# Attention scores made twice: row maxima first, then transposed scores with the maximum as a 97th row

## The reference, cut to what matters

```
q      = einsum('bld,dhk->blhk', x, Wq)             # 16 heads of 64
latent = einsum('bld,dc->blc', x, Wkv_down)         # 32 latent columns
k      = einsum('blc,chk->blhk', latent, Wk_up)
v      = einsum('blc,chk->blhk', latent, Wv_up)
attn   = einsum('bqhd,bkhd->bhqk', q, k) / sqrt(64)
attn   = softmax(where(key <= query, attn, lowest), axis=-1)
y      = einsum('bhqk,bkhd->bqhd', attn, v)
out    = einsum('bqhd,hdo->bqo', y, Wout)
```

## Time and profile before

| | |
|---|---|
| median of the runs (lowest, highest) | 3225.33 us (3221.89, 3227.55) |
| span of the profiled execution, first to last instruction | 3058.8 us |
| what lies around the span, median less span | 166.5 us |
| busy: PE, PEld, DVE, ACT, POOL | 84%, 68%, 66%, 59%, 28% |
| attention, first score matmul to last write of x | 60.8 to 1230.0 us of the span |

### The profile page before, as it was taken

One profiled execution on the slowest core, in us unless ns is written; L12 is line 12 of the kernel. 1 busy time (PEld: TensorE's weight loads), 2 busy tenths in 40 slices (PEclk: granted clock), 3 DMA queues, 4 the chain that ended last, 5 costly groups with the idle time before them and its releaser, 6 DMA issues.

```text
span 3058.8 us, 77303 instructions
## 1 busy us (share of the span) xinstructions
PE 2564.5 (84%) x26192; PEld 2090.3 (68%) x26193; DVE 2019.8 (66%) x5025; ACT 1803.4 (59%) x4422; POOL 853.6 (28%) x1042
## 2 busy tenths in 40 slices
PE   3899898989898998897997189999999987988990
PEld 2777777777777777776886166666766765776880
DVE  2677676767666776786665656666676666875664
ACT  2777777777777777563554155555556554654550
POOL 0000000000000000575566233424233224774660
PEclk9999999999999999776999598998999986768995
DMA  5221111112111210111322300000000000112225
GB/s 147 49 49 44 44 43 44 43 46 51 44 43 44 51 47 20 53 45 54 82 81 75 96 2 2 2 2 2 2 2 2 2 2 22 45 54 72 82 78 168
DMA packets 139323, 140.27 MB, mean 46 GB/s; under 512 B 30540, under 2 KB 105425, under 8 KB 138864
## 3 DMA queue, kind: packets, MB, share of 16 engines
q1 hardware_dynamic: 122096, 101.67, 13.2%
q0 software_dynamic: 16896, 34.12, 3.3%
HBM read 45.85 MB, written 40.54 MB: 28 GB/s over the span
## 4 chain that ended last, share of the span: by engine, by line
PE 55%; DVE 16%; issue 9%; ACT 9%; SPq 5%; DMA 4%; DVEq 1%; POOL 1%; ACTq 0%; POOLq 0%
PE psum L457 5%; PE psum L426 5%; PE psum L492 4%; SPq L412 3%; DVE state L1717 3%; PE psum L1514 3%; ACT probs L446 3%; PE psum L1137 3%; PE psum L1111 2%; DVE neg_max L435 2%; PE psum L1112 2%; PE psum L1562 2%; PE psum L1113 2%; DMA y<-y_tok 2%; PE psum L543 2%
## 5 line engine op out<-in xcount | busy, mean ns | idle before, releaser
L446 ACT ACTIVATE probs<-psum,neg_max 128x512 f32<-128x512 f32 (+3 forms) x1024 | 539.5, 538 | 244.7 <-DVE neg_max L435 242.6
L435 DVE TENSOR_REDUCE neg_max<-psum 128x1 f32<-128x512 f32 (+3 forms) x1024 | 457.3, 483 | 54.8 <-PE psum L427 25.8
L426 PE MATMUL psum<-ls,qs 96*128 96x512 f32 (+3 forms) x1024 | 383.6, 400 | 115.1 <-ACT probs L446 103.5
L457 PE MATMUL psum<-ident,probs 128*128 128x128 f32 x2560 | 431.4, 284 | 2.8 <-ACT probs L446 0.8
L324 POOL TENSOR_TENSOR rstd<-var_eps,half_neg 128x4 f32<-128x4 f32 x32 | 40.5, 1267 | 1115.3 <-DVE var_eps L320 1115.3
L426 PEld LDWEIGHTS psum<-ls,qs 96*128 96x128 f32 x1024 | 199.9, 195 | 219.2 <-ACT probs L446 164.3
L476 DVE COPY probs_t<-psum 128x512 f32<-128x512 f32 (+1 forms) x384 | 230.3, 600 | 147.5 <-PE psum L457 140.5
L1250 POOL DMA_INDIRECT y_tok<-yb,xb x272 | 267.3, 983 | 207.7 <-issue 116.9
L457 PEld LDWEIGHTS psum<-ident,probs 128*128 128x128 f32 x2560 | 275.9, 145 | 25.8 <-ACT probs_t L472 9.7
L914 POOL DMA_INDIRECT x_slot<-pay,pos_i x256 | 255.9, 1000 | 92.4 <-issue 77.2
L427 PE MATMUL psum<-causal_r,ident_r 128*128 128x128 f32 x1024 | 236.8, 244 | 0.0
(11 more groups left out here) (320 smaller groups left out, 6638.8 us busy)
## 6 DMA issues: line engine op xcount, KB each, us to landing
qs<-q_h SPq DMA_DIRECT2D x512, 64.0 KB, 2.0
xb<-x_slot SPq DMA_DIRECT2D x272, 66.0 KB, 1.8
qs<-q_l SPq DMA_DIRECT2D x256, 64.0 KB, 2.0
y<-y_tok SPq DMA_DIRECT2D x32, 512.0 KB, 3.8
y_tok<-yb,xb POOLq DMA_INDIRECT x272
x_sb<-in_x SPq DMA_DIRECT2D x16, 256.0 KB, 5.5
x_slot<-pay,pos_i POOLq DMA_INDIRECT x256, 2.3
out<-x_sb SPq DMA_DIRECT2D x16, 256.0 KB, 3.0
```

Of the source, the lines that this page charges most:

```text
L426: pe.matmul(o[:, at:at + n], q, ls[par][0:3 * LD, 0:n], start=(at == 0), stop=False, skip_group_check=True)
L435: last = dve.tensor_reduce(neg_max[:, par, h, qt:qt + 1], bank[u % 3][:, at:at + (qt + 1) * P], AX.X, ALU.max, negate=True)
L446: last = act.activation(probs[:, u % 3, c], bank[u % 3][:, c], ACT.Exp, bias=neg_max[:, par, h, qt:qt + 1], accum_out=row_sum[:, par, h, q ...
L457: last = pe.transpose(bank[3 + u % 2][:, c:c + P], probs[:, u % 3, c:c + P], ident[:, :])
```

## The change

The scores are now computed twice, in both orders.

- First as before, but only for the maximum: scores of unit u+20 (`AHEAD`), in two PSUM banks, without the mask matmul. One VectorE instruction adds the mask from SBUF, negates, reduces to minus the maximum, and writes the masked scores back to PSUM (L440; it is an instruction and an accumulator read).
- At (g,5) the maxima of the next group are transposed (L449), copied to SBUF (L455), and one DMA puts them into `qs` as row 96, the 97th; row 96 of `ls` is all ones.
- Then the keys-by-queries product with that row (L473, three banks) gives transposed scores less their maximum. ScalarE's exp writes them straight to `probs_t` (L483), one instruction a unit, with no bias and no row sum. GpSimd sets the masked half of each diagonal block to zero (`mask_gpsimd`, one a unit).
- The transposes of the probabilities, the copies of both engines and ScalarE's accumulator reads are gone. Values are matmuls of up to 512 columns instead of 128. Row sums come from a second such set, with ones as the stationary operand (L517). They are copied, transposed, inverted, spread out by GpSimd, transposed back and multiplied in (L530 to L562).
- The query items move to `PROJ_AT`: item 0 at (1,0), 1 at (1,2), 2 at (1,8), 3 at (2,8), 4 at (3,8), and 5 at (0,0) of the batch itself.
- Semaphores are shared where their uses do not meet, and the constants of the mask are made later. The other three stages keep their instructions.

The core of the diff:

```
-            o = bank[u % 3]
-                pe.wait_ge(s["s_exp"], b * UPS + u - 2)
+            o = bank[u % 2]
+            positive(pe, "s_max", b * UPS + u - 1)
             for qt, at in UNIT_TILES[k]:
                 n = (qt + 1) * P
-                pe.matmul(o[:, at:at + n], q, ls[par][0:3 * LD, 0:n], start=(at == 0), stop=False, ...)
-                last = pe.matmul(o[:, at + qt * P:at + n], ident_r[:, :], causal_r[:, :], start=False, stop=True, ...)
+                last = pe.matmul(o[:, at:at + n], qs[0:KEYS, h, qt * P:(qt + 1) * P], ls[par][0:KEYS, 0:n],
+                                 start=(at == 0), stop=True, skip_group_check=True)
...
+                last = dve.tensor_tensor_reduce(out=bank[u % 2][:, at:at + n], in0=bank[u % 2][:, at:at + n], in1=causal[:, L - n:L],
+                                                scale=-1.0, scalar=-MASKED, op0=ALU.add, op1=ALU.min,
+                                                accum_out=neg_max[:, g % 2, qt, j:j + 1])
...
+        def max_sync(sp, b, g):
+            sp.wait_ge(s["mx_out"], done)
+            sp.dma_start(qs[KEYS:KEYS + 1, g * HG:(g + 1) * HG, :].bitcast(F32),
+                         max_t[0:HG, :].bitcast(F32)).then_inc(s["mx_dma"], 16)
...
+        def keys_tensor(pe, b, par, u):
+            o = bank[2 + u % 3]
+            if u % GU == 0:
+                pe.wait_ge(s["mx_dma"], (b * G + h // HG + 1) * 16)
+            positive(pe, "s_exp", b * UPS + u - 2)
+            for kb, at in KEY_TILES[k]:
+                n = L - kb * P
+                last = pe.matmul(o[:, at:at + n], ls[par][0:KEYS + 1, kb * P:(kb + 1) * P], qs[0:KEYS + 1, h, kb * P:L], ...)
+            last.then_inc(s["k_mm"], 1)
...
-                last = act.activation(probs[:, u % 3, c], bank[u % 3][:, c], ACT.Exp, bias=..., accum_out=row_sum[...])
+            act.activation(probs_t[:, g % 2, j, UNIT_AT[k]:UNIT_AT[k] + UNIT_COLS[k]], bank[2 + u % 3][:, 0:UNIT_COLS[k]],
+                           ACT.Exp).then_inc(s["s_exp"], 1)
...
+            pool.affine_select(out=blocks_k, in_=blocks_k, compare_op=ALU.is_ge, fill=0.0, base=0, pattern=[[0, n], [1, P]],
+                               channel_multiplier=-1).then_inc(s["p_done"], 1)
...
+                last = pe.matmul(bank[6][j * LD:(j + 1) * LD, kb * P:L], ones_f[:, :], probs_t[:, g % 2, j, c],
+                                 start=(kb == 0), stop=(kb == QT - 1), skip_group_check=True)
...
-        PROJ_AT = {12: 0, 14: 1, 20: 2, 30: 3, 38: 4}
-        PROJ_LAST = 2
+        AHEAD = 20
+        PROJ_AT = {(0, 0): A_ITEMS - 1, (1, 0): 0, (1, 2): 1, (1, 8): 2, (2, 8): 3, (3, 8): 4}
+        MAX_AT = 5
...
             def batch(b, par, nxt, proj):
                 for u in range(UPS):
-                    if u + 2 < UPS:
-                        scores_tensor(pe, b, par, u + 2)
+                    g, v = divmod(u, GU)
+                    if u + AHEAD < UPS:
+                        scores_tensor(pe, b, par, u + AHEAD)
                     elif proj:
-                        scores_tensor(pe, b + 1, 1 - par, u + 2 - UPS)
+                        scores_tensor(pe, b + 1, 1 - par, u + AHEAD - UPS)
+                    keys_tensor(pe, b, par, u)
...
+                proj_sync(sp, b, G - 1, first=not has_back(b, 0, 1))
+                max_sync(sp, b, 1)
+                for g in range(1, G):
+                    over, g2 = next_of(g)
+                    if proj or not over:
+                        max_sync(sp, b + over, g2)
+                    if proj:
+                        proj_sync(sp, b + 1, g - 1)
```

More of the change, by code:

```diff
@@ new lines, in max_turn_tensor, with max_copy_scalar @@
+        def max_turn_tensor(pe, b, g):
+            pe.wait_ge(s["s_max"], b * UPS + (g + 1) * GU)
+            positive(pe, "mx_out", b * G + g)
+            for t in range(QT):
+                last = pe.transpose(ln_bank[0:HG, t * P:(t + 1) * P], neg_max[:, g % 2, t, :], ident[:, :])
+            last.then_inc(s["mx_mm"], 1)
+        def max_copy_scalar(act, b, g):
+            act.wait_ge(s["mx_mm"], b * G + g + 1)
+            positive(act, "mx_dma", (b * G + g) * 16)
+            act.activation(max_t[0:HG, :], ln_bank[0:HG, :], ACT.Copy).then_inc(s["mx_out"], 1)
@@ L539, in out_tensor, with sum_copy_scalar @@
-        def out_tensor(pe, b):
-            pe.wait_ge(s["y_ev2"], b * G + G)
-            for t in range(QT):
-                for g in range(G):
-                    last = pe.matmul(bank[5][:, t * P:(t + 1) * P], y_n[:, g, t * P:(t + 1) * P], wvo[:, g, :],
-                                     start=(g == 0), stop=(g == G - 1))
-            last.then_inc(s["o_mm"], 1)
+        def sum_copy_scalar(act, b, g):
+            act.wait_ge(s["sum_mm"], b * G + g + 1)
+            positive(act, "inv_mm", b * G + g)
+            act.activation(sum_t[:, :], bank[6][:, :], ACT.Copy).then_inc(s["sum_ev"], 1)
@@ new lines, in y_norm_vector, with out_tensor @@
+        def y_norm_vector(dve, b, g):
+            dve.wait_ge(s["inv_mm"], b * G + g + 1)
+            dve.wait_ge(s["y_ev"], b * G + g + 1)
+            if g == 0:
+                positive(dve, "o_mm", b)
+            dve.tensor_tensor(y_n[:, g, :], bank[6][:, :], y_t[:, :], ALU.mult).then_inc(s["y_norm"], 1)
+        def out_tensor(pe, b, t, following=1):
+            if t == 0:
+                pe.wait_ge(s["y_norm"], b * G + G)
+                pe.wait_ge(s["y_ev"], b * G + G + following)
+            for g in range(G):
+                last = pe.matmul(bank[5][:, t * P:(t + 1) * P], y_n[:, g, t * P:(t + 1) * P], wvo[:, g, :],
+                                 start=(g == 0), stop=(g == G - 1))
+            if t == QT - 1:
+                last.then_inc(s["o_mm"], 1)
```

464 lines of the change are left out of this document (232 added, 232 removed).

## The result

The changed kernel takes 3509.32 us (median of four runs, 3502.14 to 3513.90), the kernel before 3226.44 in the same measurement: ratio 1.0863, interval 1.0824 to 1.0903. It is slower by 283 us. The forecast was slower by 130, with 3355 us and a range to 3490: the sign was right, the size was not.

The account below looks back on a forecast made before the run. The kernel was taken as bound by a PE, DVE, ACT, PE loop of three banks, which the change cuts, opening query DMA waits. Batches 72.15 to 78.0 us (+82), edges +10, clock +38: +130 on 3225.3, 3355 us; range 3290 to 3460.

Parts of the forecast that it names:

- the new wait: Scores at unit 4 wait for query DMAs: 12.0 us of chain against 8 of cover, PE stands about 4.
- the half-rate rival: The fused maximum on DVE runs at half rate, 1.15 us a unit: +75 us more, 3430; chance 0.09.
- three links: Each from PE's unit (g,8) to the query DMAs' landing: copy, rest, twelve issues; 12.0 us, three a batch.
- units 4 to 8 of groups 2 and 3: PE's keys and scores, values, sums, maxima, item, mode changes and exposed loads after the landing: 7.1 us a group.
- from T to (1,0): From item 4's query DMAs landing (T), through item 5's copy and issues and group 1's maxima: 12.3 us.
- (1,0) to (1,8): PE's passes, transposes, mode changes, items 0 to 2 and a quarter of the output: 15.5 us a batch.
- The clock term: PE at 1.2 GHz after three waits: up to 5 us a batch, half under the next link; 2.5, +38 us.
- late through DVE: PE, held back by DVE after item 4's query DMAs land, is at (1,0) 12.6 us after that landing.
- Items 0 and 1: On PE between (1,0) and (1,8): item 0 0.8 us, item 1 12 x 0.11 and 1.5 waiting for copies.
- Edges: First maxima before the first keys +15 us, batch 0 -10, chain of sums at the end +5: together +10.
- Rival 1: The cover holds at unit 4's q_dma and engines set the pace: batch 64 us, -104, 3121; chance 0.17.
- Rival 3: Clock at 1.2 GHz for most of attention: +420 us at worst, 3750; in a third +140 more, 3495; chance 0.07.

Follow-up runs that it names:

- the spread kernel: Changed kernel with query items moved early, and latent items 0, 1, 2 at (0,10), (1,0), (1,2): 3096.24 us, ratio 1.0070 to the kernel before.

## Why the prediction was right and wrong

The mechanism of the new wait was right: query chain against cover, three waits a batch at unit 4 of the scores (2.5, 3.6 and 4.5 us on the mean), ScalarE and VectorE held at (0,1), starts of query copies far apart (21.8 and 21.5 us, 19 forecast). The three runs that lengthen the cover or shorten the chain show it: they take up to 13.5 us off a batch. So were the operations: the fused maximum of 512 columns takes 0.70 us and the passes go by column (0.99 for four heads of 512, with its mode change), so the half-rate rival is out:

```profile
L440 DVE CUSTOM_DVE_ANT_0 psum<-psum,causal 128x512 f32<-128x512 f32 x256 | 179.6, 701 | 245.7 <-PE psum L427 222.5 <-issue 22.7
```

The sum of a batch, forecast and measured by the table above (us):

```
                              forecast   measured
three links (1,9)-(2,3), (2,9)-(3,3), (3,9)-(0,1)   36.0   12.35 + 12.55 + 11.64 = 36.5
units 4 to 8 of groups 2 and 3                      14.2    9.59 +  9.07         = 18.7
from T to (1,0)                                     12.3                           15.8
(1,0) to (1,8)                                      15.5                           18.4
sum                                                 78.0                           89.4
clock, on top of the sum                             2.5
```

Of the 8.9 us a batch by which 80.5 fell short of 89.4:

- **The clock term is the step that failed most.** The prediction took up to 1.7 us for each of three waits, 5 a batch, and let half of it lie under the next link: 2.5. With matmuls in the waits units 4 and 5 behind (2,4) and (3,4) take 3.38 us; without them they took 5.65 and 5.13, and group 0 lost 1.7 in the same way: 5.7 us a batch, and nothing of it was seen to be hidden. These units stand ahead of the next item at unit 8, so no link runs beside them. Of the 5.7 us 3.1 came back as time, and the matmuls of that run cost 2.1 themselves. I had taken the stretch from one row, 3.5 us behind a wait of 3.2; behind these waits it is up to 6.8. Group 1 has 3.2 us at half clock in (1,2) and (1,3), behind a wait of 1.6; its units 3 to 5 take 5.63 instead of the 4.88 of the spread kernel, 0.75 that may be the clock too. That makes 3.2 to 4.0 of the 8.9, the largest part but not half.
- **The wait for the maximum at (0,4)** is dearer than "late through DVE": unit (0,3) takes 2.6 us instead of 1.5 of the spread kernel, at either clock, 1.1. From T to (1,0) another 0.7 has no cause shown.
- **Items 0 and 1** were 2.2 us too cheap, by what is left of (1,0) to (1,8): (1,0) to (1,2) took 7.9 us. TensorE's loads wait some 1.8 us for VectorE's rest of the latents each time (26.3 us in 15 waits), with all of its queue behind it; part of the 2.2 can be the half clock in (1,2).
- **Links** were within 0.6 each, 0.5 in all, and units 4 to 8 without the clock within 0.3 each, 0.4 in all. "Hidden" was right for exps, masks and POOL's copy.
- **Edges**: +38.6 us, not +10. First exp +17.9 (15 forecast), batch 0 +10.1 (I had it at -10), the last batch +3.3, the tail +7.3 (5).
- Together 14 x 17.25 = 241 and 38.6 are the 280 by which x is written later, against 82 + 38 + 10. So 125 of the 150 us that were missing are in the batches, the rest in the edges, the second term that was mis-sized.
- **Rival 1** would not have given 64 either: with the cover there (early, then spread items) a batch is 76.7 and 72.2. A dense group is 15.5 us, not 12.6 (why is open, as said above), and the change then stands level with the kernel before. What it takes from VectorE and ScalarE it gives to TensorE: 5.1 us a group of value and sum passes, and scores and keys twice.
- **Rival 3**, the clock, got too small a chance: 25.8 us of the 89.4 of a batch are at half clock, near its "third", though they cost less than its 140 us. Its 3750 does not follow from the +420 beside it either, which makes 3775.

## What to carry to other kernels

When a value is needed earlier than before, look for the chain that makes it, and count DMAs by their issues on their queue: twelve issues of 0.6 us were the link here, and moving the item five or six units up was worth near 6% where all the saved engine time was worth nothing. Price a new wait of all engines twice, once as itself and once as the slower TensorE behind it. Matmuls that fill a wait to keep the clock up have a price when they outlast it. Before setting a span against a median, look whether both come from one set of runs.

## What was not expected of the hardware

- The same code takes 5% more in some sets of runs than in others: 1830 and 1997 us for the stages behind the attention, nothing for the attention itself. What it hangs on is open.
- A kernel with a fifth of its attention's matmuls left out ran no faster than with them (1.0114 against 1.0070 and 0.9969), with a granted clock of 0.87 against 0.93 and 0.95. The cause is not shown.
- ScalarE's DMA issues take 0.6 us each and its next exp stands behind them, 4.0 us for six.
